# Two token halves side by side in TensorE's array, in the head of a selective-scan layer

## The reference

```
xz = layer_norm(x) @ W_in ; u, z = split(xz)
uc = silu(causal_conv4(u) + conv_b)            # 256 channels
dbc = uc @ W_x                                 # 8 + 16 + 16 columns
dt_r, Bs, Cs = dbc[:8], dbc[8:24], dbc[24:40]
dt = softplus(dt_r @ W_dt + b_dt)              # 256 channels
h  = h * exp(dt * A) + (dt * uc) * B_t         # 16 states per channel, over time
y  = sum_states(h * C_t) + uc * Dskip
out = x + (y * silu(z)) @ W_out
```

## Time and profile before

| what | us |
|---|---|
| median of 3 runs | 657.6 (657.42 to 659.01) |
| the profiled execution, its own time | 656.44 |
| its span | 654.7 |
| mean granted TensorE clock | 0.961 |
| busy: PE, PEld | 574.4, 467.2 |
| busy: DVE, ACT, POOL | 452.1, 384.8, 361.6 |
| first scan starts | 68.17 |

### The profile page before, as it was taken

One profiled execution on the slowest core, in us unless ns is written; L12 is line 12 of the kernel. 1 busy time (PEld: TensorE's weight loads), 2 busy tenths in 40 slices (PEclk: granted clock), 3 DMA queues, 4 the chain that ended last, 5 costly groups with the idle time before them and its releaser, 6 DMA issues. The chain is left out here.

```text
span 654.7 us, 10842 instructions
## 1 busy us (share of the span) xinstructions
PE 574.4 (88%) x3876; PEld 467.2 (71%) x3876; DVE 452.1 (69%) x798; ACT 384.8 (59%) x751; POOL 361.6 (55%) x306
## 2 busy tenths in 40 slices
PE   5999877899999998997887897588999888889997
PEld 2444676899998996766557676588788876776676
DVE  6797898999989996982857981333333466647663
ACT  3678889779799774563676964022221124746670
POOL 0588788989889782885505607704702460223530
PEclk9999799899999999898998998778999889989999
DMA  4034134345544412000610016103313010000002
GB/s 126 4 93 76 35 71 92 71 105 110 101 102 106 98 24 73 1 2 13 183 27 2 6 29 151 54 5 93 103 31 78 17 34 1 1 1 2 2 0 65
DMA packets 43230, 35.77 MB, mean 55 GB/s; under 512 B 11895, under 2 KB 32297, under 8 KB 43178
## 3 DMA queue, kind: packets, MB, share of 16 engines
q1 hardware_dynamic: 42154, 32.99, 21.3%
q0 software_dynamic: 1024, 2.10, 1.1%
HBM read 28.98 MB, written 6.09 MB: 54 GB/s over the span
## 5 line engine op out<-in xcount | busy, mean ns | idle before, releaser
L891 DVE TENSOR_TENSOR_SCAN l0s_ring<-l_XM,l0s_ring,bank 128x512 f32<-128x512 f32 x96 | 114.5, 1257 | 5.3 <-ACT l_XM L602 4.4
L602 ACT ACTIVATE l_XM<-l_DT,l_negA 128x512 f32<-128x512 f32 x120 | 79.7, 712 | 10.2 <-DVE l0s_ring L891 10.0
L749 POOL TENSOR_TENSOR l0s_ring<-l0s_ring,l0s_c_rest 128x1024 f32<-128x1024 f32 x32 | 65.8, 2058 | 18.2 <-DVE l0s_ring L891 8.3
L749 POOL TENSOR_TENSOR l0s_ring<-l0s_ring,all_XF 128x1024 f32<-128x1024 f32 x31 | 66.5, 2148 | 7.9 <-DVE l0s_ring L891 5.5
L449 PE MATMUL bank<-all_ident,l0s_ring 128*128 128x128 f32 x512 | 66.6, 275 | 0.0
L449 PEld LDWEIGHTS bank<-all_ident,l0s_ring 128*128 128x128 f32 x512 | 58.7, 142 | 0.0
L2046 POOL DMA_INDIRECT all_XNT<-gy,all_slot x16 | 15.6, 974 | 35.5 <-DMA gy<-l1s_ys 31.2
L418 PE MATMUL bank<-all_ident,all_XNT 128*128 128x128 f32 x256 | 33.8, 274 | 1.0 <-DVE l0s_ring L891 0.7
L332 PE MATMUL bank<-l_XM,l_wins 128*128 128x512 f32 x64 | 31.1, 631 | 0.9 <-ACT l_XM L546 0.9
L625 ACT ACTIVATE all_XNT<-all_OUTF,l_wins 128x256 f32<-128x256 f32 x72 | 30.5, 495 | 0.2
L418 PEld LDWEIGHTS bank<-all_ident,all_XNT 128*128 128x128 f32 x256 | 28.8, 141 | 2.0 <-DVE l0s_ring L891 0.9
(11 more groups left out here) (454 smaller groups left out, 1649.4 us busy)
## 6 DMA issues: line engine op xcount, KB each, us to landing
l0s_c_rest<-bc_rows SPq DMA_DIRECT2D x16, 512.0 KB, 5.1
all_XF<-bc_rows SPq DMA_DIRECT2D x16, 512.0 KB, 4.9
l_wall<-in_L_ffn_W SPq DMA_DIRECT2D x14, 256.0 KB, 4.5
all_X<-in_L_attn_x SPq DMA_DIRECT2D x4, 256.0 KB, 3.7
gx<-l1m_TD SPq DMA_DIRECT2D x1, 1024.0 KB, 6.1
gy<-l1m_TD SPq DMA_DIRECT2D x1, 1024.0 KB, 8.6
out<-all_X SPq DMA_DIRECT2D x4, 256.0 KB, 2.3
gy<-l1s_ys SPq DMA_DIRECT2D x7, 128.0 KB, 1.8
```

Source lines behind the costliest of these rows:

```text
L602: nc.scalar.activation(dst, DT[:, j, block_of(n)], ACT.Exp, scale=negA[:, j, n % DS:n % DS + 1]).then_inc(decay_ready, 1)
L749: nc.gpsimd.tensor_tensor(hc[n % CRING][:, :, :], h(n)[:, :, :], wide(c_wide[p % HRING][:, n % 2, :]), ALU.mult).then_inc(hc_ready, 1)
L891: nc.vector.tensor_tensor_scan(h(n)[:, j, :], factor, added, before, ALU.mult, ALU.add).then_inc(h_ready, 1)
```

## The change

Each block's 512 tokens are cut into two halves of 256 (HBLK), g = 0 and 1. DBC is now 104 partitions by 1024: half g lies at partitions 64 g to 64 g + 39, and the blocks follow each other in 256 columns each. W_dt is loaded twice, at partitions 0 and 64. project writes half g to partitions 64 g of bank 4 (the two column parts of the array), step_size reads it from there (two row parts) and writes columns 256 g of banks 6 and 7. keep_dbc, store, spread and turn_b follow the new layout. The diff, without lines that only change the number waited for on proj_loaded (96 to 112):

```diff
+HALF, HBLK = P // 2, BLK // 2
...
-        DBC = big.sb("DBC", [DR + 2 * DS, T])
+        DBC = big.sb("DBC", [2 * HALF + DR + 2 * DS - HALF, T // 2])
...
-        wdt = big.sb("wdt", [DR, DI])
+        wdt = big.sb("wdt", [HALF + DR, DI])
...
+            half = lambda b, g: slice(b * BLK + g * HBLK, b * BLK + (g + 1) * HBLK)
+            dbc = lambda g, rows, b: DBC[g * HALF:g * HALF + rows, bass.ts(b, HBLK)]
...
-                        sp.dma_start(bc_rows[:, blk(b)], DBC[DR:DR + 2 * DS, blk(b)]).then_inc(bc_stored[b], 16)
+                        for g in range(2):
+                            sp.dma_start(bc_rows[:, half(b, g)], DBC[g * HALF + DR:g * HALF + DR + 2 * DS, bass.ts(b, HBLK)]).then_inc(bc_stored[b], 16)
...
-                            sp.wait_ge(bc_stored[2 * p // DS], 16)
+                            sp.wait_ge(bc_stored[2 * p // DS], 32)
...
-                    sp.dma_start(wdt[:, :], W["L0_attn_W_dt"]).then_inc(proj_loaded, 16)
+                    for g in range(2):
+                        sp.dma_start(wdt[g * HALF:g * HALF + DR, :], W["L0_attn_W_dt"]).then_inc(proj_loaded, 16)
...
                         for j in range(JT):
-                            last = nc.tensor.matmul(S.bank[4][0:DR + 2 * DS, :], wx[:, j, :], UC[:, j, blk(b)], start=(j == 0), stop=(j == JT - 1))
+                            for g in range(2):
+                                last = nc.tensor.matmul(S.bank[4][g * HALF:g * HALF + DR + 2 * DS, 0:HBLK], wx[:, j, :], UC[:, j, half(b, g)],
+                                                        start=(j == 0), stop=(j == JT - 1))
                         last.then_inc(dbc_done, 1)
 
                     def step_size(b):
                         pe.wait_ge(dbc_ready, b + 1)
-                        for j in range(JT):
-                            if b:
-                                pe.wait_ge(max_ready, JT * (b - 1) + j + 1)
-                            nc.tensor.matmul(S.bank[6 + j][:, :], wdt[:, j * P:(j + 1) * P], DBC[0:DR, blk(b)], start=True, stop=True).then_inc(dt_done, 1)
+                        if b:
+                            pe.wait_ge(max_ready, JT * b)
+                        for i, (j, g) in enumerate(((0, 0), (1, 1), (0, 1), (1, 0))):
+                            if i >= 2:
+                                pe.wait_ge(dt_done, 2 * JT * b + i - 1)
+                            nc.tensor.matmul(S.bank[6 + j][:, g * HBLK:(g + 1) * HBLK], wdt[g * HALF:g * HALF + DR, j * P:(j + 1) * P], dbc(g, DR, b),
+                                             start=True, stop=True).then_inc(dt_done, 1)
...
-                        nc.tensor.matmul(bank_b[:, :], row, DBC[:, block_of(n)], start=True, stop=True).then_inc(b_spread, 1)
+                        for g in range(2):
+                            if g:
+                                pe.wait_ge(b_spread, 2 * number(n) + 1)
+                            at = g * HALF
+                            row = S.ident[at:at + DR + 2 * DS, at + DR + n % DS:at + DR + n % DS + 1].broadcast_to([DR + 2 * DS, P])
+                            nc.tensor.matmul(bank_b[:, g * HBLK:(g + 1) * HBLK], row, dbc(g, DR + 2 * DS, n // DS), start=True, stop=True).then_inc(b_spread, 1)
...
-                        for t in range(TILES):
-                            last = nc.tensor.transpose(bank_t[:, t * BC:(t + 1) * BC], DBC[0:BC, bass.ts(t, P)], S.ident[0:BC, 0:BC])
-                        last.then_inc(b_turned, 1)
+                        for g in range(2):
+                            if g:
+                                pe.wait_ge(b_turned, 1)
+                            at = g * HALF
+                            for b in range(NBLK):
+                                for k in range(2):
+                                    t = b * TPB + 2 * g + k
+                                    last = nc.tensor.transpose(bank_t[:, t * BC:(t + 1) * BC], DBC[at:at + BC, b * HBLK + k * P:b * HBLK + (k + 1) * P],
+                                                               S.ident[at:at + BC, at:at + BC])
+                            last.then_inc(b_turned, 1)
...
-                        nc.scalar.activation(DBC[:, blk(b)], S.bank[4][0:DR + 2 * DS, :], ACT.Copy).then_inc(dbc_ready, 1)
+                        for g in range(2):
+                            last = nc.scalar.activation(dbc(g, DR + 2 * DS, b), S.bank[4][g * HALF:g * HALF + DR + 2 * DS, 0:HBLK], ACT.Copy)
+                        last.then_inc(dbc_ready, 1)
...
-                            act.wait_ge(dt_done, JT * b + j + 1)
+                            act.wait_ge(dt_done, 2 * JT * b + JT + j + 1)
...
-                        act.wait_ge(b_turned, 1)
+                        act.wait_ge(b_turned, 2)
...
-                        dve.wait_ge(b_spread, number(n) + 1)
+                        dve.wait_ge(b_spread, 2 * number(n) + 2)
```

More of the change, by code:

```diff
@@ L347, in project @@
                         pe.wait_ge(u_ready, JT * (b + 1))
-                        pe.wait_ge(proj_loaded, 96)
+                        pe.wait_ge(proj_loaded, 112)
                         if b:
@@ L376, in spread @@
                     def spread(n):
-                        row = S.ident[0:DR + 2 * DS, DR + n % DS:DR + n % DS + 1].broadcast_to([DR + 2 * DS, P])
                         if n == 0:
@@ L551, in silu_u @@
                         if b == 0 and j == 0:
-                            act.wait_ge(proj_loaded, 96)
+                            act.wait_ge(proj_loaded, 112)
                         nc.scalar.activation(UC[:, j, blk(b)], S.bank[j][:, :], ACT.Silu, bias=conv_b[j]).then_inc(u_ready, 1)
```

## The result

The changed kernel takes 0.9959 of the time of the kernel before (95% interval 0.9946 to 0.9971), about 2.7 us less by that ratio and 2.3 by the medians, 656.7 and 659.0 us, each of 18 runs on one chip. Twelve more runs of the changed kernel on another chip gave 0.9977 (0.9951 to 1.0002), so by the total alone a gain is clear of the noise in the first comparison and just not in the second. The profiled execution took 653.84 us, its span is 652.1, against 656.44 and 654.7.

The account below looks back on a forecast made before the run. TensorE was taken to lead in the head with ScalarE close behind, VectorE in the scan loop. Head savings less keep_dbc's and spread's costs put the loop 2.8 us early: 657.6 - 2.8 = 654.8 us, range 653.3 to 659.5.

Parts of the forecast that it names:

- the sum: Head savings and costs added in order to the scan loop's start: 2.8 us early, time 654.8 us.
- Project, column parts: Project in each of four blocks: eight instructions in five slots of 0.213 = 1.07 us, saving 0.64 per block.
- rival (a): Parts in project and step_size fully overlap: 0.86 and 0.5 us saved per block, 654.0 us; chance 0.08.
- Step_size, row parts: Step_size in each block: partial overlap with two waits, 1.60 us against 1.91, saving 0.31 per block.
- ScalarE binds at project(2): Project(2) in the head starts with ScalarE's silu, 1.54 us early, not TensorE's 1.90.
- Keep_dbc: ScalarE's copy in each block: two activations of 256 columns for one of 512, +0.05 us, bounds 0 and +0.13.
- Spread: Spread before the first scan: two halves with a wait between, 1.49 us against 1.16, +0.33.
- The walk: Through the head: keep_dbc(3) 3.08 us early, the first scan 2.70, the second step and loop 2.8.
- turn_b: Turn_b at the loop's start: one more wait and 0.2 us later start, costing nothing; 0.5 without its cover.
- an earlier dip: Granted clock's drop at 70 to 75 us might come in 60 to 70, matmuls there taking up to twice as long.
- The DMAs: Doubled stores and one more W_dt load: bc_rows fetches 0.3 us later, costing nothing, at most 0.3.
- rival (d): Project's column parts don't overlap and their loads are exposed: 2.64 us, +0.93 per project, 661.7 us; chance 0.15.

Follow-up runs that it names:

- part-order run: Project's matmuls issued part 0 then part 1, without a wait, against the changed kernel: project 1.00 us, stage 223.33 and 223.57 us, ratio 0.9964 to the kernel before.
- the kernel with the transposes: Seven identity transposes added behind project(3) in TensorE's idle time, against the changed kernel: stage 223.30 and 223.26 us, ratio 0.9972 to the kernel before.

## Why the prediction was right, and where it was not

The forecast was 2.8 us less, the stage lost 2.79 and the time 2.7 (2.3 by the medians). The mechanism was right, but so close an agreement is luck: up to positive(3) the head gained 0.7 more than forecast, and the clock's early fall, for which the sum has nothing, took 0.7 back. With the first error alone 3.5 would have been saved, with the second alone 2.1.

- **Project, column parts**: 1.84 was to become 1.2 by five slots, it became 0.99. The slots were wrong: I let the high and low instruction of a matmul hold back the other part. The saving is 0.85 per block and not 0.64, in effect rival (a)'s 0.86; in the part-order run not even the program's order held them back.
- **Step_size, row parts**: 1.60 forecast, 1.42 measured, 0.49 saved and not 0.31, from the same error. The wait cost what was said: the second pair starts 0.75 after the first (40.06, 40.81), where the working has 0.76 before the load.
- **ScalarE binds at project(2)**: right. TensorE waited 0.53 for its silu there (47.76), and what step_size(1) saved went into that wait.
- **Keep_dbc**: +0.05 forecast, +0.19 measured, beyond the bound of 0.13. I took the overlap of two copies from 69.48 and 69.75; two copies at different partitions follow each other at 0.40, 0.38 long each, with none.
- **Spread**: 1.49 forecast; measured 1.49 too, from 61.87 to VectorE's 63.36.
- **The walk**: keep_dbc(3) 3.82 early against 3.08 (rival (a) 3.9), the first scan 3.31 against 2.70, positive(3) 3.48 against 2.8. Up to here rival (a) was the nearer one (3.65 at the loop).
- **turn_b**: "At nothing; with that cover gone, 0.5" is the step that failed. With spread(2) and turn_b at half clock the cover was not enough: ScalarE waited 2.49 for turn_b, VectorE's wait at step 3 grew from 0.98 to 1.69, and 0.7 was given back. I had counted an earlier dip within the spread and not as a term; it is a term of 0.7, since the kernel with the transposes, where the clock falls 3.4 us later, has 0.70 of it back.
- The DMAs cost nothing, as said, and the loop is as long as before (from step 3 to the FFN phase 171.7 us in both kernels).

The slower rival (d), exposed loads, is out: project would have taken 2.64 and took 0.99, too little for eight loads of 0.117 beside four slots of 0.21. The Trainium skill (TensorE: Matmul & The Clock Gate, Part 3) says a load overlaps only with matmuls of other row groups; here both parts use all 128 rows, and the measurement decides against it. Nor does its rule that matmuls start strictly in the queue's order fit the part-order run, which took 1.00 us where that order would need at least three slots of 0.43, unless the chip's queue has another order than the program.

## What to carry to other kernels

Where a matmul leaves half of the array empty, two token halves in two parts can run together, in fp32 too: with 40 columns project went from 1.84 to 0.99 us, and with 8 rows and a wait between the pairs step_size went from 1.91 to 1.42. In project the halves need not alternate in the program. The halves then come out at other partitions: copy them with one activation over all partitions, since two copies in turn cost twice (0.77 us against 0.39). After a gain on TensorE, look at where its clock now falls: here it fell 7 us earlier, and what stood behind it at half speed took back a fifth of the gain.

## What the runs showed of the hardware that was not expected

- Project in part order lasted 1.07 us against 1.06 (x8): its instructions start two by two, so the second part's matmuls didn't wait for the first part's, which stood ahead of them in the program.
- A copy of 104 x 256 on ScalarE lasts 0.39 us, one of 40 x 256 0.38; two of the latter take 0.77 together.
- The stage's length repeats to 0.05 us over executions and chips in three kernels (226.79 and 226.78, 224.00 and 223.95, 223.30 and 223.26) and to 0.24 in a fourth (project in part order), while the median totals of the kernel before were 659.0, 656.7, 631.8 and 631.7 us. In its two profiles that difference lies in the phases behind the stage (404 and 381 us).
